# One more batch of attention ahead of the feed-forward, in a gated block kernel on one core

## What is computed

```
x = x + tanh(g_xattn) * attention(layernorm(x), ctx)   # 16 heads of 32, causal, Wq, Wkv, Wout
x = x + tanh(g_ffn) * ffn(layernorm(x))

ffn:  qx = fp8(xr / scale_x)                 # rows of x, each by its own largest value / 448
      g, u = qx @ fp8(Wgate).T, qx @ fp8(Wup).T      # 512 -> 1408, with the scales put back
      t = silu(g) * u
      qt = fp8(t / scale_t)
      y = qt @ fp8(Wdown).T                  # 1408 -> 512
```

## Times and profile before

| | us |
|---|---|
| median of three launches | 823.28 |
| their lowest and highest | 823.01, 824.52 |
| the profiled launch | 827.38 |
| span of the profiled execution | 825.6 |

### The profile page before, as it was taken

How to read it: one execution, slowest core, us unless ns; L and a number is a source line. 1 busy time by engine, 2 the same in 40 slices (tenths; PEclk the granted TensorE clock), 3 DMA queues, 4 the chain that set the end, 5 groups by cost and what they waited for, 6 DMA issues and landing times.

```text
span 825.6 us, 15682 instructions
## 1 busy us (share of the span) xinstructions
PE 708.6 (86%) x6142; PEld 437.2 (53%) x6142; DVE 699.9 (85%) x1206; ACT 550.8 (67%) x971; POOL 418.9 (51%) x534
## 2 busy tenths in 40 slices
PE   1335585999999999999999999999999999988854
PEld 1324363656565666666666565666665666643421
DVE  6985553899999999999999998989898989997774
ACT  3576463877778686868686868686868685845340
POOL 2665343455546464646464646373737373625441
PEclk9999597999999999999999999999999999998985
DMA  8339779375756566565657676666666655541203
GB/s 294 110 89 138 156 96 142 53 133 96 138 104 131 112 113 129 105 136 104 136 97 140 94 143 96 137 97 134 107 130 107 130 101 109 93 84 36 62 13 86
DMA packets 146852, 93.10 MB, mean 113 GB/s; under 512 B 113755, under 2 KB 118875, under 8 KB 146779
## 3 DMA queue, kind: packets, MB, share of 16 engines
q1 hardware_dynamic: 143386, 85.94, 55.0%
q0 software_dynamic: 1808, 5.77, 2.7%
q10 hardware_dynamic: 1584, 0.39, 0.5%
HBM read 31.86 MB, written 8.40 MB: 49 GB/s over the span
## 4 chain that ended last, share of the span: by engine, by line
DVE 42%; ACT 25%; PE 13%; POOL 7%; DMA 6%; issue 6%; SPq 0%; POOLq 0%; DVEq 0%
ACT PT L1148 10%; DVE mx L1478 8%; PE pair L642 6%; ACT room L1183 5%; DVE room L1339 4%; DVE mx L1477 4%; ACT room L1171 3%; DVE rsum L1482 3%; DVE cx L1525 3%; DVE x L1502 3%; DMA Q<-ql 2%; DVE amax L1508 2%; ACT L1148 2%; POOL x L549 2%; POOL room L545 2%
## 5 line engine op out<-in xcount | busy, mean ns | idle before, releaser
L527 POOL TENSOR_SCALAR_AFFINE_SELECT PT<-PT 128x512 f32<-128x512 f32 x128 | 87.1, 695 | 64.0 <-ACT PT L1148 62.9
L545 POOL TENSOR_TENSOR room<-room,up_scale 128x512 f32<-128x512 f32 (+1 forms) x96 | 111.6, 1183 | 10.9 <-ACT room L1171 10.8
L1148 ACT ACTIVATE PT<-pair 128x768 f32<-128x768 f32 x128 | 97.7, 822 | 0.2
L642 PE MATMUL pair<-WdT,room 128*128 128x512 bf16 x352 | 85.2, 393 | 11.0 <-DMA room<-room 11.0
L642 PE MATMUL pair<-WgT,room 128*128 128x512 bf16 (+1 forms) x384 | 87.3, 369 | 4.7 <-DMA room<-room 4.7
L1171 ACT ACTIVATE room<-room,sx 128x512 f32<-128x512 f32 (+1 forms) x96 | 65.4, 682 | 37.5 <-DVE room L1554 33.7
L642 PE MATMUL pair<-WuT,room 128*128 128x512 bf16 (+1 forms) x384 | 90.4, 366 | 0.0
L1157 ACT ACTIVATE cx<-x,sum 128x512 f32<-128x512 f32 x32 | 23.1, 722 | 100.0 <-DVE x L1502 100.0
L642 PE MATMUL pair<-xT,WqTh 128*128 128x256 bf16 x512 | 87.4, 273 | 0.2 <-DVE room L1569 0.2
L1478 DVE TENSOR_REDUCE mx<-pair 128x2 f32<-128x512 f32 x128 | 87.2, 681 | 0.0
L549 POOL TENSOR_TENSOR x<-room,x 128x512 f32<-128x512 f32 x32 | 40.7, 1271 | 79.4 <-DVE room L1604 79.4
(11 more groups left out here) (135 smaller groups left out, 1829.7 us busy)
## 6 DMA issues: line engine op xcount, KB each, us to landing
xin<-in_x_dram SPq DMA_DIRECT2D x16, 512.0 KB, 4.1
K<-kh SPq DMA_DIRECT2D x32, 256.0 KB
Q<-qh SPq DMA_DIRECT2D x32, 256.0 KB
x<-in_x_dram SPq DMA_DIRECT2D x16, 512.0 KB, 4.6
out_dram<-x SPq DMA_DIRECT2D x16, 512.0 KB, 3.3
K<-kl SPq DMA_DIRECT2D x16, 256.0 KB
Q<-ql SPq DMA_DIRECT2D x16, 256.0 KB
room<-in_L_ffn_w_down_dram SPq DMA_DIRECT2D x4, 704.0 KB, 6.6
```

The costliest lines, as they stand in the source:

```text
L527: pool.affine_select(out=view, in_=view, compare_op=ALU.is_ge, fill=0.0, base=0, pattern=[[0, 2], [0, 2], [1, P]], channel_multiplier=-1). ...
L545: pool.tensor_tensor(g, g, up_scale[:, chunk(n)[1]], ALU.mult).then_inc(slw_done, 1)
L642: last = pe.matmul(out_ap, lhs, rhs, start=(fresh and n == 0), stop=(n == len(terms) - 1), skip_group_check=not fresh)
L1148: act.activation(head_columns(ring(b, c), 0, 384), head_columns(shifted_pair[c][:, :], 0, 384), ACT.Exp, scale=SCALE).then_inc(exp_done, 1)
```

## The change

No operation is added and none is left out. Three things change.

First, the offsets. In iteration k PE now makes scores, turned maxima, shifted pairs 0 to 6 and weighted(0) of batch k + 2, keys and queries of k + 3, and shifted(7), weighted(1) to weighted(3) and projected of k + 1, beside the feed-forward of k and down of k - 1. The loops of the other engines follow. So attention runs one batch further ahead of the feed-forward, and batch 1's attention comes before feed-forward 0.

Second, every table of banks is new, and with it the waits. `gate_products(b, 3)` and `(b, 4)` now wait for the maxima 6 and 8 of batch b + 2, where before the third and fourth waited for the turned rows and for a gate of the same batch.

Third, the order inside all five loops is new: in SP's loop the transfers of the scales move, in POOL's and DVE's the weights' units.

```diff
-        score_pair = (pairs[2], pairs[1], pairs[0], pairs[1], pairs[0], pairs[1], pairs[0], pairs[1])
+        score_pair = (pairs[0], pairs[1], pairs[3], pairs[2], pairs[3], pairs[1], pairs[3], pairs[2])
...
-        wo_bank = (bank[6], bank[0])
-        gate_bank = (bank[5], bank[1], bank[2], bank[0], bank[1], bank[6])
-        up_bank = (bank[7], bank[2], bank[3], bank[0], bank[1], bank[3])
+        wo_bank = (bank[0], bank[0])
+        gate_bank = (bank[2], bank[6], bank[5], bank[2], bank[5], bank[6])
+        up_bank = (bank[1], bank[6], bank[4], bank[0], bank[1], bank[0])
...
             def gate_products(b, n):
                 if n == 0:
                     pe.wait_ge(qxT_in[0], 16 * b + 16)
-                if n == 0 and b < 14:
-                    pe.wait_ge(kl_done, 2 * b + 5)
                 if n == 1 and b < 15:
-                    pe.wait_ge(max_done, 8 * b + 15)
-                if n == 2 and b < 15:
-                    pe.wait_ge(max_done, 8 * b + 16)
+                    pe.wait_ge(rsum_done, b + 2)
+                if n == 2 and b < 14:
+                    pe.wait_ge(v_done, 2 * b + 5)
                 if n == 3:
                     pe.wait_ge(qxT_in[1], 16 * b + 16)
-                if n == 4:
-                    pe.wait_ge(gs_done, 6 * b + 2)
-                if n == 5 and b < 15:
-                    pe.wait_ge(mT_done, b + 2)
+                if n == 3 and b < 14:
+                    pe.wait_ge(max_done, 8 * b + 22)
+                if n == 3 and b >= 14:
+                    pe.wait_ge(gs_done, 6 * b + 1)
+                if n == 4 and b < 14:
+                    pe.wait_ge(max_done, 8 * b + 24)
...
             def projected(b, i):
...
-                if i == 2 and b < 15:
-                    pe.wait_ge(max_done, 8 * b + 11)
+                if i == 2:
+                    pe.wait_ge(x1_done, 2 * b + 1)
...
-                at(k + 1, scores, 0)
+                at(k + 2, scores, 0)
...
-                at(k + 2, keys, 0)
+                at(k + 3, keys, 0)
...
-                if k == -2:
-                    scales_out(0)
+                if k == -4:
+                    scales_out(0)
...
```

More of the change, by code:

```diff
@@ L938, in _ @@
-                at(k, projected, 1)
-                if k == -4:
-                    attention_weights(6)
-                at(k, projected, 2)
-                at(k, projected, 3)
-                at(k + 1, scores, 3)
-                at(k + 2, keys, 0)
-                at(k + 2, keys, 1)
-                at(k + 1, scores, 4)
-                at(k + 2, queries, 0)
-                at(k - 1, down, 1)
-                if k == -8:
-                    attention_weights(0)
-                at(k + 1, scores, 5)
@@ new lines, in _ @@
+                at(k + 1, projected, 0)
+                if k == -2:
+                    unit_turned(13)
+                at(k + 2, scores, 4)
+                if k == -3:
+                    unit_turned(9)
+                if k == -6:
+                    attention_weights(1)
+                if k == -5:
+                    unit_turned(3)
+                at(k + 2, scores, 5)
+                at(k, up_products, 0)
+                at(k + 1, projected, 1)
+                at(k + 2, scores, 6)
@@ new lines, in _ @@
+                at(k + 2, scores, 7)
+                at(k, gate_products, 3)
+                at(k + 3, keys, 0)
+                at(k + 3, keys, 1)
+                at(k, gate_products, 4)
+                at(k + 3, queries, 0)
+                at(k + 2, turned_maxima)
+                at(k + 3, keys_rest, 0)
+                at(k, up_products, 1)
+                if k == -2:
+                    unit_turned(14)
+                at(k + 3, queries, 1)
+                at(k, up_products, 2)
+                if k == -4:
+                    attention_weights(5)
@@ new lines, in _ @@
+                at(k + 1, projected, 2)
+                at(k + 3, keys_rest, 1)
+                at(k + 3, queries_rest, 0)
+                if k == -5:
+                    attention_weights(2)
+                if k == -4:
+                    attention_weights(6)
+                at(k, gate_products, 5)
+                at(k + 2, shifted, 0)
+                if k == -4:
+                    unit_turned(7)
+                    unit_turned(8)
+                at(k + 3, queries, 2)
+                at(k + 1, projected, 3)
@@ new lines, in _ @@
+                if k == -5:
+                    attention_weights(3)
+                at(k + 2, shifted, 1)
+                at(k + 3, queries, 3)
+                at(k - 1, down, 1)
+                if k == -8:
+                    unit_turned(0)
+                at(k + 2, shifted, 2)
+                if k == -3:
+                    unit_turned(10)
+                if k == -4:
+                    attention_weights(7)
+                if k == -3:
+                    attention_weights(9)
+                at(k + 2, shifted, 3)
```

1208 lines of the change are left out of this document (560 added, 648 removed).

## The result

The changed kernel took 853.1 us (851.34 to 854.38, four launches) against 823.9 for the one before in the same comparison: a ratio of 1.0346 (1.0312 to 1.038). The forecast was 812.5, with a range of 803 to 826 and "faster" at 0.75; "slower" had 0.18. The profiled launch took 853.27, its span is 851.5.

A forecast was written before the change was run, and what follows sets the result against it. PE was taken to bound the middle, with its idle time in fill and tail. Terms of -22 - 6.6 - 2.2 + 20 = -10.8 took the span from 825.6 to 814.8, scaled to a median of 812.5; range 803 to 826.

The forecast's parts named there:

- the fill: Start up to sums(2), DVE's row-sum reciprocal of batch 2: at 197 against 218.94, gain 22, between 6 and 28.
- the sum of the middle: Twelve periods at 41.7, 500.4 in all, gain 6.6; loop over DVE and PE of 40.9, under PE's 41.5.
- Rival A: Middle: DVE makes maxima late, so PE's fourth and fifth gate chunks stand; periods of 43, median 828; chance 0.12.
- (a): Fill: scores(0) starts at 88 against 93.37, as POOL issues the w_up gather some 6 us earlier.
- (b): Fill: scores(1) starts at 125 against 136.90, with one scale writing left in the queue, as in batch 0.
- (c): Fill: sums(1), DVE's row-sum reciprocal of batch 1, follows scores(1) by 32.5, at 157.5.
- (d): Fill: from batch 1's row-sum reciprocal to batch 2's takes 39.5, between 36.8 and 42.1, so the latter is at 197.
- The tail and the stretch before it: Stretch between the last two row-sum reciprocals 41.5, gain 2.2; tail after it 76 against 55.97, loss 20.
- rival C: Tail: three stretches of about 2.5 at half PE clock, 7.5 longer, 820; sign: granted clock below 0.9; chance 0.06.
- Rival B: Fill unchanged: a scale writing holds Q, DVE's roundings hold scores(0); sums(2) at about 209, median 824.5; chance 0.14.
- D: Middle and fill gain more than counted: periods of 41.2 and sums(2) at 190, median 800; chance 0.07.
- E: First gates wait for batch 1's attention anyway; fill and tail cancel, middle unchanged, 822; chance 0.03.

The follow-up runs named there:

- m2: Changed kernel with the two turning transfers of x moved on SP ahead of the loads of x and x1 and turn_qx 1: 832.23 us.
- m3: Changed kernel with the unread outputs of means1 and squares1 sent to a tile of their own, orders untouched: 833.76 us.
- f2: Changed kernel with unit 14's scales, floor and lift on DVE moved behind unit 11's last rounding: 848.6 us.
- x1: Changed kernel with turning transfers of x first and the three scale writings replaced by one-row copies of x (outputs wrong): 812.03 us.
- x2: Kernel before with the three scale writings replaced by one-row copies of x (outputs wrong): 807.59 us.
- v3: Kernel before with scales turned on DVE in 32 x 32 blocks, then written in 128 pieces of 128 bytes, readers unchanged: 808.4 us.
- v4: Changed kernel with turning transfers of x first, unit 14 behind unit 11's rounding, and scales turned on DVE before writing: 811.37 us.
- v1: Kernel before with weight scales written in 128 pieces, 44 (or 16) bytes each, and readers stepping at a stride of 11 (or 4): 840.24 us.

## Why the prediction was wrong

The span came out 36.7 above the forecast: 16.2 in the fill, 21.9 in the middle, 2.8 less in the stretch after it and 1.3 more in the tail.

**The step that failed first is the sum of the middle.** It counted a loop over PE and DVE and PE's own list (41.5), and left out ScalarE, POOL and SP, though the change reordered all five. (The terms of the loop on DVE add up to 15.9 and not to 15.7, so the loop is 41.1 and not 40.9; that was not what failed.) Three things that were open to see closed a second loop: in the new order the turning transfers stand behind two loads of 512 KB, `means1` stands 2 us behind them and not 14, and silu 2 and the parts of the maxima stand behind it. m2 and m3 show this loop to be the loss of the middle: with it a period is 44.25 to 43.0, and without it most are 41.97, 0.3 above what I had taken.

**Rival A** was nearest in the middle (periods of 43, against 43.5 on average) and had the wrong cause: PE waits for DVE's maxima 0.8 us, once, in all twelve periods. What it waits for are the parts that POOL makes of them, late by a way over ScalarE and a transfer that A did not have. Its 828 was 25 too low all the same, as it left the fill at its gain.

**(a)** failed. The gather was to be issued some 6 us earlier and was issued 0.7 earlier: POOL comes to it only after a rounding of its own, which waited for DVE (0.63 at 64.38) and takes 2.13. And the moved roundings lie behind the gather on DVE (f2: 5.6 us). I had taken the order on POOL's list for a time, and had not followed what DVE has between the landing and unit 11.

**(b)** scores(1) came 35.7 after scores(0) for a forecast of 37, but not for its reasons. PE did not wait for Q any more; it stood for 4.3 in the stop. So that this term came within 1.3 is luck. That the writings were dear was right, and undersized: I gave one of them 6.3 with the load of x1, and all three cost 16 to 20 (x1, x2). **(c)** and **(d)** came out 2.8 long each (35.3 and 42.3); DVE stood idle 7.5 before sums(1) with no releaser, and PE's first gate in feed-forward 0 waited 6.64 for a turning of qx that took 11.6 behind the third writing.

**The tail and the stretch before it** came out within 1.3 and 2.8, but the tail in part by luck, since **rival C**, the clock, did come. Its sign was a granted clock under 0.9 between the last two feed-forwards: it was 0.78 from 792 to 798, 0.50 from 816 to 822 and 0.66 from 822 to 828. Three halves of down ran slow in the new tail, 4.24, 4.87 and 4.88 us after standstills of 4.76, 3.58 and 9.28, against 2.54 for the others; in the old one two did (4.87 and 4.21). That is some 2.4 more, where C had 7.5 and the forecast nothing. So the rest of the tail came out about 1 under the count, and the two errors nearly cancel. The Trainium skill, "TensorE: Matmul & The Clock Gate", section 'Part 1: The HAM clock gate (the "warmup" mystery)', makes the throttled state the default, which activity lifts; the trace agrees in direction: the halves behind standstills are the slow ones. Over the whole tail the granted clock was 0.84, before 0.76, with PE busy 46.2 of 77.3 and 32.2 of 56.0, so the mean alone would have hidden it.

**Rival B** had the fill within 4 us (209 for 213), with the middle on top. Of its two causes, DVE's roundings did hold scores(0) (f2), and the writings did cost, but through the stops and not through a wait for Q. **D** (800) and **E** (822, the middle unchanged) did not come.

The small pieces: the Trainium skill, "DMA: Bandwidth & Descriptors", section "Rules for kernel authors", says that a non-contiguous last dimension is lowered to one descriptor per element, and to rearrange it so that it is contiguous. The runs agree in direction and add a size: two writings of 5.5 KB in 1408 pieces of 4 bytes and one of 2.0 KB in 512, against three of 16 KB in 128 pieces of 128 bytes, are 16 us of 824 (v3).

## What to carry to other kernels

Where a change reorders every engine, walk the loop that each wait closes, on the engines with slack and on the transfer queues too. Here the distance on the new list between the issue of a transfer and the first step that waits for it, and what stands behind that step, would have pointed at the loss, which two lines of SP's order mend. A step that only writes something unread into a shared tile can carry a wait; give it a tile of its own. Work put ahead at the start is owed at the end: against v3, v4 won 11.9 us in the fill and 4.9 in the stretch before the tail, and lost 21.5 in the tail.

## What the hardware showed that I had not expected

A write of 5.5 KB in 1408 elements took some 14 us from issue to landing, where 128 pieces of 44 bytes took 3.7 (v1), and it cost others more than that: with the three writings gone, sums(2) of the kernel before came 15.3 us earlier (x2), and in x1 the stops of PE and DVE without a releaser (4.3 and 6 us in the changed kernel, 1.2 on PE in m2) were gone with them. Reading a float32 scale at a stride of 11 elements, in an operation whose other operands were cut into runs of 128 elements for it, made a DVE product with a PSUM operand 1.54 times as long (692 to 1069 ns), and a stride of 4 a similar one 1.55 times (746 to 1155 ns). A 32 x 32 block transpose of 128 x 32 float32 took 206 ns. POOL's same instructions took longer in the new order (the causal cut 836 ns on average against 695 in the kernel before); what runs beside them changed, but no run tells what of it does this, and it cost nothing measurable (m2).
